# Agent attention in a decoder: token scores and mixing in four column bands of TensorE

## The reference, cut to what matters

```python
qkv = einsum('bnc,dc->bnd', layernorm(x), w_qkv); q, k, v = three parts of 256 channels
agent = einsum('bnc,c->bn', q, w_conv1)
agent_attn = softmax(einsum('bn,bnc->bc', agent * 256 ** -0.5, k), axis=-1)     # over channels
agent_v = softmax(einsum('bc,bnc->bn', agent_attn, v), axis=-1)                 # over tokens
agent_v = einsum('bn,bnc->bc', agent_v, v)
x = x + softmax(agent[:, :, None], axis=-1) * agent_v[:, None, :]
```

## Time and profile before

| | us |
|---|---|
| median of 3 runs | 3015.07 |
| lowest, highest of them | 3014.1, 3028.93 |
| the profiled execution's own time | 3029.68 |
| its span | 3027.9 |
| TensorE busy | 2686.9 (89% of the span) |
| VectorE busy | 2008.4 (66%) |
| ScalarE busy | 1517.9 (50%) |
| mean granted TensorE clock | 0.931 |

### The profile page before, as it was taken

One profiled execution on the slowest core, in us unless ns is written; L12 is line 12 of the kernel. 1 busy time (PEld: TensorE's weight loads), 2 busy tenths in 40 slices (PEclk: granted clock), 3 DMA queues, 4 the chain that ended last, 5 costly groups with the idle time before them and its releaser, 6 DMA issues. The chain is left out here.

```text
span 3027.9 us, 60052 instructions
## 1 busy us (share of the span) xinstructions
PE 2686.9 (89%) x20638; PEld 1752.0 (58%) x20639; DVE 2008.4 (66%) x4550; ACT 1517.9 (50%) x2982; POOL 459.2 (15%) x482
## 2 busy tenths in 40 slices
PE   6899999986799999999786689999999799969993
PEld 3344444443476767666665357777777655556662
DVE  2699999897377777777543457777777456653334
ACT  2666666662366666666342146666666233302222
POOL 0000000000200000000042111111110033224441
PEclk9899999997899999999877789999999799969997
DMA  4000000000000000000000100000000210001125
GB/s 113 0 1 0 0 0 0 0 0 20 21 22 20 20 20 15 20 20 11 7 8 1 40 16 21 20 22 23 20 20 11 70 64 19 20 21 63 62 64 165
DMA packets 57928, 80.55 MB, mean 27 GB/s; under 512 B 8880, under 2 KB 47058, under 8 KB 57490
## 3 DMA queue, kind: packets, MB, share of 16 engines
q1 hardware_dynamic: 51778, 62.69, 7.2%
q0 software_dynamic: 6048, 16.52, 1.7%
HBM read 63.59 MB, written 15.60 MB: 26 GB/s over the span
## 5 line engine op out<-in xcount | busy, mean ns | idle before, releaser
L1146 DVE CUSTOM_DVE_ANT_0 xa_h_scores<-xa_h_score_bank,xa_h_added 112x375 f32<-112x375 f32 x1024 | 518.1, 544 | 148.4 <-PE xa_h_score_bank L1081 132.6
L1240 ACT ACTIVATE xa_h_probs<-xa_h_scores,xa_h_negmax 112x375 f32<-112x375 f32 x1024 | 561.4, 600 | 0.9 <-DVE xa_h_negmax L1153 0.6
L1093 PEld LDWEIGHTS xa_h_turn_bank<-keep_ident,xa_h_probs 112*125 112x125 f32 x3072 | 398.6, 190 | 91.2 <-DVE xa_h_probs_t L1160 22.2
L1093 PE MATMUL xa_h_turn_bank<-keep_ident,xa_h_probs 112*125 112x112 f32 x3072 | 438.5, 280 | 8.8 <-DVE xa_h_probs_t L1160 8.5
L1160 DVE COPY xa_h_probs_t<-xa_h_turn_bank 125x448 f32<-125x448 f32 x512 | 319.0, 623 | 150.6 <-PE xa_h_turn_bank L1093 137.5
L1246 ACT ACTIVATE xa_h_probs_t<-xa_h_turn_bank 125x448 f32<-125x448 f32 x256 | 138.6, 541 | 304.0 <-PE xa_h_turn_bank L1093 304.0
L679 DVE TENSOR_TENSOR_SCAN mb_state<-mb_decay,mb_drive 128x1792 f32<-128x1792 f32 x64 | 249.4, 3897 | 0.8 <-ACT mb_decay L613 0.2
L1081 PE MATMUL xa_h_score_bank<-xa_h_keys,xa_h_queries 32*112 32x375 f32 x2048 | 231.8, 522 | 11.2 <-DVE xa_h_row_max L1146 10.6
L474 PE MATMUL mb_y_bank<-mb_read_out,keep_ident 128*128 128x448 f32 x448 | 203.3, 602 | 34.0 <-DVE mb_read_out L695 23.7
L1106 PEld LDWEIGHTS xa_h_sums_bank<-xa_h_probs_t,xa_h_values 125*32 125x32 f32 x6144 | 142.0, 110 | 154.2 <-DVE xa_h_probs_t L1160 149.1
L1106 PE MATMUL xa_h_sums_bank<-xa_h_probs_t,xa_h_values 125*32 125x112 f32 x6144 | 202.7, 265 | 14.4 <-issue 6.0
(11 more groups left out here) (342 smaller groups left out, 4151.3 us busy)
## 6 DMA issues: line engine op xcount, KB each, us to landing
xa_context<-in_ctx_t SPq DMA_DIRECT2D x64, 375.0 KB, 3.1
lm_w<-in_m_w SPq DMA_DIRECT2D x16, 512.0 KB, 9.9
lm_e_wide<-lm_result_rows SPq DMA_DIRECT2D x8, 896.0 KB, 9.5
keep_x<-in_x SPq DMA_DIRECT2D x4, 896.0 KB, 15.8
lm_latent_rows<-lm_rows SPq DMA_DIRECT2D x8, 448.0 KB, 3.2
out_x<-keep_x SPq DMA_DIRECT2D x8, 448.0 KB, 6.0
xa_mask_raw<-in_key_mask SPq DMA_DIRECT2D x1, 1312.5 KB
mb_f_pw<-in_pw SPq DMA_DIRECT2D x1, 1024.0 KB
```

What stands on the lines that cost most here:

```text
L1093: last = pe.transpose(turn_bank[(par + kc) % 2][0:KP, g * S:(g + 1) * S], probs[par][:, g, kc * KP:(kc + 1) * KP], keep.ident[0:S, 0:S])
L1146: dve.tensor_tensor_reduce(scores[par][:, g, :], score_bank[g][0:S, 0:SK], added[s][:, :], 1.0, -BIG, ALU.add, ALU.max, row_max[par][:, g: ...
L1240: act.activation(probs[par][:, g, :], scores[par][:, g, :], ACT.Exp, bias=negmax[s][:, G * c + g:G * c + g + 1]).then_inc(probs_ready, 1)
```

## The change

Batch b = 4g + r goes to column band r, the rows 32r to 32r + 31 of the bank. The matmuls are issued group by group, with the four bands innermost; within a band the diagonal weights still put batch b into row b of 32. The other rows of a band hold zeros. So the scores lie on 128 rows, of which 32 matter, and so do the softmax, its transpose (now with 128 columns), the mix and its transposes. The copy to `weights_wide` reads column 32r + 4g + r of 128, the copy to `gathered` reads 128 columns per chunk and need not repeat 32. `weights_wide` is 112 x 1056, where it was 112 x 1024, so that the diagonal can be addressed in one pattern; the statistics of the two softmaxes have tiles of their own. The numbers of matmuls, of transposes, of copies and of waits are as before, and no wait is added.

```diff
-        channel_wide, weights_wide = sb("channel_wide", [128, DC, B, B]), sb("weights_wide", [S, B, B])
-        token_exp, token_probs = sb("token_exp", [B, S]), sb("token_probs", [B, S])
-        stat = sb("stat", [B, 8])
-        gathered, agent_v = sb("gathered", [128, DC, 4, B]), sb("agent_v", [128, D])
+        channel_wide, weights_wide = sb("channel_wide", [128, DC, B, B]), sb("weights_wide", [S, GROUPS * 4 * (B + 1)])
+        token_exp, token_probs = sb("token_exp", [4 * B, S]), sb("token_probs", [4 * B, S])
+        key_stat, token_stat = sb("key_stat", [B, 4]), sb("token_stat", [4 * B, 4])
+        gathered, agent_v = sb("gathered", [128, DC, 4 * B]), sb("agent_v", [128, D])
...
-            for b in range(B):
+            for g in range(GROUPS):
                 for c in range(DC):
-                    last = pe.matmul(banks[0:B, 0, 0:S], channel_wide[:, c, b, :], tokens_t[:, c, b // G, b % G * S:(b % G + 1) * S],
-                                     start=b == 0 and c == 0, stop=b == B - 1 and c == DC - 1)
+                    for r in range(G):
+                        last = pe.matmul(banks[B * r:B * (r + 1), 0, 0:S], channel_wide[:, c, G * g + r, :], tokens_t[:, c, g, r * S:(r + 1) * S],
+                                         start=g == 0 and c == 0, stop=g == GROUPS - 1 and c == DC - 1)
             last.then_inc(pe_step, 1)
             pe.wait_ge(dve_step, 4)
-            pe.transpose(banks[0:S, 1, 0:B], token_probs[:, :], keep.ident[0:B, 0:B]).then_inc(pe_step, 1)
+            pe.transpose(banks[0:S, 1, 0:4 * B], token_probs[:, :], keep.ident[:, :]).then_inc(pe_step, 1)
             pe.wait_ge(act_step, 5)
-            for b in range(B):
-                last = pe.matmul(banks[0:B, 2, 0:D], weights_wide[:, b, :], tokens[:, b, :], start=b == 0, stop=b == B - 1)
+            for g in range(GROUPS):
+                for r in range(G):
+                    b = G * g + r
+                    last = pe.matmul(banks[B * r:B * (r + 1), 2, 0:D], weights_wide[:, B * b:B * (b + 1)], tokens[:, b, :],
+                                     start=g == 0, stop=g == GROUPS - 1)
             last.then_inc(pe_step, 1)
             pe.wait_ge(act_step, 6)
             for c in range(DC):
-                last = pe.transpose(banks[:, 1, c * B:(c + 1) * B], mixed[:, c * 128:(c + 1) * 128], keep.ident[0:B, 0:B])
+                last = pe.transpose(banks[:, 1, c * 4 * B:(c + 1) * 4 * B], mixed[:, c * 128:(c + 1) * 128], keep.ident[:, :])
...
-            act.activation(token_exp[:, :], banks[0:B, 0, 0:S], ACT.Exp, bias=stat[:, 4:5], accum_out=stat[:, 5:6]).then_inc(act_step, 1)
+            act.activation(token_exp[:, :], banks[:, 0, 0:S], ACT.Exp, bias=token_stat[:, 0:1], accum_out=token_stat[:, 1:2]).then_inc(act_step, 1)
             act.wait_ge(pe_step, 5)
-            act.activation(weights_wide[:, :, :].rearrange("p b j -> p (b j)")[:, 0:B * B:B + 1], banks[0:S, 1, 0:B], ACT.Copy).then_inc(act_step, 1)
+            act.activation(weights_wide[:, :].rearrange("p (g i) -> p i g", g=GROUPS)[:, 0:G * (B + 1):B + 1, :],
+                           banks[0:S, 1, 0:G * (B + 1)].rearrange("p (r i) -> p r i", r=G)[:, :, 0:B:G], ACT.Copy).then_inc(act_step, 1)
             act.wait_ge(pe_step, 6)
-            act.activation(mixed[:, :], banks[0:B, 2, 0:D], ACT.Copy).then_inc(act_step, 1)
+            act.activation(mixed[:, :], banks[:, 2, 0:D], ACT.Copy).then_inc(act_step, 1)
             act.wait_ge(pe_step, 7)
-            act.activation(gathered[:, :, :, :], banks[:, 1, 0:DC * B].rearrange("p (c b) -> p c b", c=DC).unsqueeze(2).broadcast_to([128, DC, 4, B]),
-                           ACT.Copy).then_inc(act_step, 1)
+            act.activation(gathered[:, :, :], banks[:, 1, 0:DC * 4 * B].rearrange("p (c b) -> p c b", c=DC), ACT.Copy).then_inc(act_step, 1)
...
-            softmax(banks[0:B, 0, 0:S], token_exp[:, :], token_probs[:, :], 4)
+            softmax(banks[:, 0, 0:S], token_exp[:, :], token_probs[:, :], token_stat, False)
```

More of the change, by code:

```diff
@@ L1375, in switch_and_agent @@
         token_sum, key_probs_t = (sb(n, [128, DC, B]) for n in ("token_sum", "key_probs_t"))
-        key_exp, key_probs, mixed = (sb(n, [B, D]) for n in ("key_exp", "key_probs", "mixed"))
-        channel_wide, weights_wide = sb("channel_wide", [128, DC, B, B]), sb("weights_wide", [S, B, B])
-        token_exp, token_probs = sb("token_exp", [B, S]), sb("token_probs", [B, S])
-        stat = sb("stat", [B, 8])
-        gathered, agent_v = sb("gathered", [128, DC, 4, B]), sb("agent_v", [128, D])
+        key_exp, key_probs, mixed = sb("key_exp", [B, D]), sb("key_probs", [B, D]), sb("mixed", [4 * B, D])
+        channel_wide, weights_wide = sb("channel_wide", [128, DC, B, B]), sb("weights_wide", [S, GROUPS * 4 * (B + 1)])
+        token_exp, token_probs = sb("token_exp", [4 * B, S]), sb("token_probs", [4 * B, S])
+        key_stat, token_stat = sb("key_stat", [B, 4]), sb("token_stat", [4 * B, 4])
+        gathered, agent_v = sb("gathered", [128, DC, 4 * B]), sb("agent_v", [128, D])
         own, own_inverse, own_probs, own_wide = sb("own", [S, B]), sb("own_inverse", [S, B]), sb("own_probs", [S, 4, B]), sb("own_wide", [128, GROUPS, S])
@@ L1506, in _ @@
             for c in range(DC):
-                last = pe.matmul(banks[:, 3, 0:D], gathered[:, c, :, :].rearrange("p r b -> p (r b)"), wv_t[:, c, :], start=c == 0, stop=c == DC - 1)
+                last = pe.matmul(banks[:, 3, 0:D], gathered[:, c, :], wv_t[:, c, :], start=c == 0, stop=c == DC - 1)
             last.then_inc(pe_step, 1)
@@ L1573, in _ @@
             act.wait_ge(dve_step, 1)
-            act.activation(key_exp[:, :], banks[0:B, 0, 0:D], ACT.Exp, bias=stat[:, 0:1], accum_out=stat[:, 1:2]).then_inc(act_step, 1)
+            act.activation(key_exp[:, :], banks[0:B, 0, 0:D], ACT.Exp, bias=key_stat[:, 0:1], accum_out=key_stat[:, 1:2]).then_inc(act_step, 1)
             act.wait_ge(pe_step, 2)
@@ L1599, in _ @@
             pool.memset(channel_wide[:, :, :, :], 0.0).then_inc(wide_cleared, 1)
-            pool.memset(weights_wide[:, :, :], 0.0).then_inc(wide_cleared, 1)
+            pool.memset(weights_wide[:, :], 0.0).then_inc(wide_cleared, 1)
             pool.wait_ge(loaded, weights.count)
@@ L1699, in scales, with softmax @@
                 dve.scalar_tensor_tensor(shift2[:, here], moments2[:, here, 0], -1.0, rstd2[:, here], ALU.mult, ALU.mult).then_inc(scales_ready, 1)
[L1701 to L1710, removed]
+            def softmax(source, exps_of, probs, stat, first):
+                dve.wait_ge(pe_step, 1 if first else 4)
+                dve.reduce_max(stat[:, 2:3], source, AX_X).then_inc(small_step, 1)
+                dve.wait_ge(small_step, 1 if first else 3)
+                dve.tensor_scalar(stat[:, 0:1], stat[:, 2:3], -1.0, None, ALU.mult).then_inc(dve_step, 1)
+                dve.wait_ge(act_step, 1 if first else 4)
+                dve.reciprocal(stat[:, 3:4], stat[:, 1:2]).then_inc(small_step, 1)
+                dve.wait_ge(small_step, 2 if first else 4)
+                dve.tensor_scalar(probs, exps_of, stat[:, 3:4], None, ALU.mult).then_inc(dve_step, 1)
             dve.memset(ones[:, :], 1.0).then_inc(constants, 1)
@@ L1730, in _ @@
             dve.tensor_tensor(own[:, :], agents, agents, ALU.subtract).then_inc(own_step, 1)
-            softmax(banks[0:B, 0, 0:D], key_exp[:, :], key_probs[:, :], 0)
+            softmax(banks[0:B, 0, 0:D], key_exp[:, :], key_probs[:, :], key_stat, True)
             dve.wait_ge(own_step, 2)
```

## The result

| | before | changed |
|---|---|---|
| median, us | 3028.87 (9 runs) | 3005.53 (9 runs) |
| lowest to highest | 3014.1 to 3035.05 | 2997.99 to 3010.47 |
| profiled execution: own time, span | 3029.68, 3027.9 | 2998.6, 2996.8 |

The ratio is 0.9933, with a 95% interval of 0.9914 to 0.9952: 20.3 us less on 3028.87 (14.5 to 26.0). It agrees with the averages of the nine runs each, 3024.8 and 3004.6 us; the two medians alone lie 23.3 us apart. The median of before is 13.8 us above the 3015.07 that stood in the prediction, since six more runs came to the first three and five of the six lie near the upper end.

A forecast was written before the change was run, and what follows sets the result against it. TensorE's token scores and mixing were taken to bound the tail, nothing else being under way. Savings of 9.1 and 10.3 us less 0.2 and 0.3 made 18.9, so 3015.07 became 2996 us, range 2989 to 3009.

The forecast's parts named there:

- The bound: Token scores and mixing in the tail: TensorE sets the time, 14.20 and 15.69 us, and the kernel loses what they lose.
- Scores: Token scores: 128 passes become 32 waves, 14.2 to 5.1 us, 9.1 us saved, bounds 7.9 and 10.7.
- Mixing: Mixing: 16 waves with the clock falling again, 15.7 to 5.4 us, 10.3 us saved, bounds 8.7 and 12.1.
- What gets dearer: Softmax on 128 rows and transposes of 128 columns: +0.2 us together, 0.05 to 0.5.
- Behind the mixing: L1507 and the first L1515 burst could meet the lower clock: +0.3 us taken, up to +1.2.
- Sum: Whole kernel: -9.1 - 10.3 + 0.2 + 0.3 = -18.9 us.
- The absolute time: Whole kernel: the median 3015.07 less 18.9 gives 2996 us, own bounds 3000 and 2992.
- A: Both blocks and more of the next stage: the clock stays at 0.50; 3003 us, chance 0.09.
- B: Both blocks: the weight loads of a wave queue up and set the pace; 3007 us, chance 0.04.
- rival C: Whole kernel: saving is there, but measured executions lie in the upper part of the spread; 3010 us, chance 0.12.
- D: Both blocks: bands don't overlap here at all; 3016 us, chance 0.02.
- E: Both loops: changing band makes TensorE finish each pass first, 27.6 us more; 3043 us, chance 0.03.

The follow-up runs named there:

- before_shifted: The kernel before with 6 more score-form matmuls (12 passes) ahead of the scores, into an unused bank: mixing 14.00 us, first score pass to first add 34.6 us.
- scores_only: The changed kernel with the mixing back in one band, its copies and transposes on 32 rows: ratio to the kernel before 0.9966, mixing 14.00 us.
- after_shifted: The changed kernel with 40 more matmuls (80 passes) in four bands ahead of the scores, into an unused bank: mixing 5.35 us.
- band_outermost: The changed kernel with the same matmuls reordered, all of one band before the next in both loops: scores 12.55 us, mixing 13.16 us.

## Why the prediction was right

- **The bound.** The two blocks were on the path in full: taken alone they took 11.1 and 10.2 us off the stretch, and the kernel followed with 10.3 and 11.8 us (5.4 to 15.1 and 5.7 to 18.2).
- **Scores, forecast 5.1 us.** Measured 4.46, 5.02 and 5.01. The two later traces have the clock rising 3.6 us into the block, as assumed; in the first it rose after 2.48. The wave costs one single pass, and at 1.00 a little less than forecast: 0.104 us from the burst of L1106 has the start-up of the burst in it, and the last starts of the changed kernel lie 0.096 us apart.
- **Mixing, forecast 5.4 us.** Measured 3.66, the lower bound. This is the term that was mis-sized, by 1.7 us. The step was "the busy stretch ahead of this gap is shorter, so I expect the fall again and sooner". The runs show that the length of the busy stretch doesn't order it: with a pause of 2.0 to 2.2 us the clock fell behind scores of 14.2, 12.6 and, with the added passes, 6.4 us, and held behind 14.9 (before_shifted), 11.1 and 4.5 to 5.1. All traces agree with its going by how long after the last rise the mixing came: 3.6 to 4.2 us after it, where the changed kernel has it, the clock held. No row of the kernel before showed this ahead of the result. The cost of a wave of 256 columns, for which no row of the same form stood, is that of a single pass: 15 x 0.217 + 0.38 = 3.6. At the same clock, 1.00, one band takes 14.00 us (scores_only) and four bands 3.66, a factor of 3.83.
- **What gets dearer, forecast +0.2 us.** The pause grew by 0.18 us (2.04 to 2.22), of which 0.09 is the transpose, and from the end of the mixing to the first add it went from 3.61 to 3.79 us, 0.14 of it in the pair of transposes. Together 0.36 us, inside 0.05 to 0.5.
- **Behind the mixing, forecast +0.3 us.** L1507's successor took 1.13 us as before, since the clock held; nothing was lost. The rounds of VectorE still come every 2.56 us.
- **Sum.** Forecast 18.9 us, the tail gave 21.4 (20.8 in the other traces), the comparisons of the whole 20.3 and 20.6 (0.0068 of 3025.53). In the first trace the 2.5 us more are 1.7 in the mixing, 0.6 in the scores and 0.3 not spent behind them, less 0.2 for the wider steps.
- **The absolute time.** 2996 was forecast and 3005.53 came. The base was at fault: 3015.07 was a median of three runs, two of them at the low end of a spread of 21 us. The forecast's own bounds, 3000 and 2992, missed it. It lies in the wider range, 2989 to 3009, only because that was drawn over rivals A and B, and neither came; that the time fell inside is luck, the saving isn't. 3028.87 less the forecast 18.9 would be 3010. That is rival C's number, and its argument, that half of the known executions lay in the upper part, deserved more than a term in the range.
- **The rivals.** The weight loads of a wave don't queue up (B): 128 loads of 0.110 us or more, at least 14.1 us of loading, ran within 4.2 us. So the rule of the Trainium skill, "TensorE: Matmul & The Clock Gate", "What overlaps and what doesn't", that a load overlaps a running matmul only in another row group, doesn't hold for column bands here; the trace goes against it. Nor did it hold within one band: in the 10.58 us of single passes at 1.00 before the change, passes were under way for 10.58 and loads for 10.34, all on the same 128 rows. The prediction named L1106 alone against the rule, and gave its loads 128 rows where the earlier trace rows has 125. D and E fell with the first trace. A didn't come: the clock rose in the scores in all three traces and held in the mixing, and the stage behind was never longer than before.

## What to carry to other kernels

Where a loop of matmuls has 32 output rows each, give neighbours in program order different column bands: with 112 and with 256 columns streamed, four float32 matmuls then took the time of one, weight loads included, at no cost but wider steps behind them (0.36 us here). Fewer rows than 32 weren't tried. The order need not be strict, two matmuls in a row per band cost 0.07 us a block, four nearly half the gain and eight most of it, so put the band in the inner loops. When the change is worth about as much as the spread of the executions, forecast a ratio and take the stretch from two traces; a median of three runs was off by 14 us.

## What the runs showed of the hardware that was not expected

- **A band holds four passes.** Visits of 2 and 4 passes a band overlap in full (15 intervals for 64 passes of the mixing, 3.66 and 3.73 us); visits of 8 took 8.17 us and of 16 13.16. In the visits of 8 passes and more, the last four of one visit ran beside the first four of the next. What holds them, and whether it is four passes or two float32 matmuls, these kernels can't tell apart.
- **The clock's fall went with the moment.** Behind the same pause of 2.0 to 2.2 us it fell in five traces and held in seven. A mixing 1.6 us later against the last rise of the clock (before_shifted), or 1.9 to 2.5 us later (after_shifted), turned it round, one trace each. A fall cost 1.7 us each time (3.66 to 5.35, 14.00 to 15.69). In the mixing of band_outermost too it lasted 3.4 us.
- **Where the executions spread.** The stage of the first cross attention, from the layer norm ahead of it to the one behind it (starts of L199), took 760.1 to 760.4 us in nine of the thirteen traces, 753.5 to 753.8 in three and 757.0 in one, whatever the kernel. The longer ones had 47 us at clock 0.50 in it, the one of 757.0 had 33.5, the shortest 27 to 30. The time ahead of that stage lay between 746.8 and 751.8 us. Of the 31.1 us between the first two traces, 6.6 are this stage. Part of it is a stretch at 0.50 near its end, 20 us long in the first trace of before and 7 in that of the changed kernel; why it differs wasn't tried.
